# Counting edges with packed bank numbers and one-hots on ScalarE, and five steps of the graph part put in another order

## The chip, the cores and the metric

One core of one Trainium2 chip runs the whole program. The metric is the device time in microseconds, the median of the runs; lower is better. The engines of the core work on queues of their own and meet at semaphores: TensorE (PE, its weight loads PEld), VectorE (DVE), ScalarE (ACT), GpSimd (POOL), and SyncE (SP), which here only starts DMAs.

## The reference, cut to what matters

Four graph networks run one after the other on 512 nodes of width 768 and 8704 edges, each inside a residual sum and a layer norm:

```python
edge_index = jnp.stack([src, dst])
x = _layernorm(x + gat(x, 8 heads, then 1 head, edge_index))           # L0: attention on edges
x = _layernorm(x + rgat(x, edge_index, edge_type_3))                   # L1: 3 relations, 4 heads, then 1
x = _layernorm(x + rgcn(x, edge_index, edge_type_4))                   # L2: 3 layers, 4 relations
x = _layernorm(x + gcn(x, edge_index))                                 # L3: 2 layers
return x
```

In L0 a head computes `h = x @ W`, `e = leaky_relu(alpha_s[src] + alpha_d[dst])`, a softmax of e over the edges of each dst, and sums `h[src] * alpha` per dst. In L2 a relation's messages are divided by its in-degree: `norm = where(etype == r, 1 / max(deg[dst], 1), 0)`.

## The kernel before

The kernel never touches single edges after its first part. **Counting** (`count_and_weigh`, up to 106 us) turns the edge list into matrices that say how many edges of each kind go from source node to destination node. All later sums over edges are dense products with these 512 x 512 matrices.

Counting sorts the edges by source into 8 buckets of 64 sources and pads each bucket to chunks of 128 edges, 75 chunks in all (`CHUNKS`). For each chunk VectorE makes two one-hot matrices: `key_first` (128 edges x 128 keys, a piece of 15 chunks at a time, L382) and `dst_hot` (128 edges x 512 destinations, one chunk at a time, L433). TensorE multiplies them (L554) and adds the product to the PSUM bank of the chunk's bucket. Which bank that is depends on the data: VectorE counts it (L395 to L399) into `bank_i`, and TensorE's queue loads the numbers into registers, 8 at a time (`load_banks`, L535 to L540), each load four matmuls ahead of its use. There are three such rounds (`count_round`) over the same `dst_hot`, with other keys. Only the first waits for `dst_hot`, chunk by chunk. Between rounds ScalarE copies banks 0 to 4 and VectorE 5 to 7 out of PSUM (`tally`), and TensorE clears them with products of zeros (L543). During the rounds ScalarE does nothing else. A few late additions on VectorE (`total`, `most`) run beside round 3.

**The graph part** (`graph_layers`) begins with x transposed by TensorE (L1009). VectorE first copies six banks of the last round out (four named by `first_read`), then, in `turn`, subtracts ScalarE's rounded copy from each of six transposed pieces (`turn_hi`, `turn_lo`), so that a float32 product can be made of three products of rounded halves. The first product (L975, `product`) wants these. SyncE waits for all four `first_read` before it loads the second weight pass and stores `tally`.

Weights come in passes of three pieces. SyncE loads a piece into `w_raw` once POOL is done with the same piece of the pass before (`w_low`); ScalarE copies it rounded into `w_pair` (`split_high`), POOL subtracts (`weights_low`, L891). Each engine does its list in the written order, so a ScalarE copy of a tile waits behind a `split_high` whose load has not landed.

At the end of the first eight products TensorE transposes the largest count (`most`, L1192) into bank 7 for a flag that VectorE reads.

A **head** of L0 (`head`): TensorE makes the rows of the next head (8 products) and in between turns the source terms (`turn_source`, L989, bank 6), spreads them over partitions (`spread_source`, L993, bank 7), and, once VectorE has the maxima and the terms u and v (`uv_ready`), turns and spreads those (L984, L996, L997). Then it sums the probabilities (L1104) and makes six aggregations (L1114, 12 products of 512 columns each for the rounded and rest parts of rows and probabilities), each read by VectorE through a normalization and an elu. In the first head `late_weights` (L1027, L1038) stands in place of the output product, and `turn_late_weights` (L1061: 12 products of 8 columns) comes ahead of the aggregations. It waits for `wk_lo` of VectorE. ScalarE waits for its result before the elu copies. The eighth head has no next rows: its small steps stand between the chunks of the seventh head's output product (`eighth_head`, `out_by_chunk`, L1137), `source` after chunk 0 and `spread` after chunk 2 of 0 to 5, the turning of u and v after all.

In **L2** relation r's edge sums (L1535, L1543; `edge_sums`) are scaled by 1 over the in-degree. VectorE sums the rows of the count matrix (`count_sum`, three additions into `r_den`), TensorE sums over partitions (L1569, `degrees`), VectorE transposes and inverts it. For relation r + 1 the sum stands behind relation r's six tiles (`edge_tiles`, L2674) and behind the low part of the counts (`count_low`). ScalarE loads the next count matrix over the old one (`load_count`) once both are done, and splits the next two weight passes after that, before the copies of the next relation's tiles (`edge_high`). The edge sums use two PSUM banks and two `xt` buffers in turn.

## Time and profile before

| what | us |
|---|---|
| median of 3 runs (1712.0 to 1712.7) | 1712.49 |
| the profiled execution, its own time | 1713.1 |
| its span, first to last instruction | 1711.3 |
| TensorE busy | 1645.9 (96%) |
| VectorE busy | 1086.5 (63%) |
| ScalarE busy | 665.3 (39%) |
| GpSimd busy | 649.9 (38%) |
| mean granted clock of TensorE, as a share of full | 0.984 |

The profile is of one execution. Times in it count from the first instruction. A matmul's duration is longer than its pitch, since matmuls overlap; what one costs is the distance to the next start. Idle time is put down to the instruction that ended it.

### The profile page before, as it was taken

How to read it: one execution, taken by the hardware profiler on the slowest of the kernel's cores; microseconds unless marked ns; L12 is line 12 of the kernel's file. 1: busy time of each engine (PE TensorE's matmuls, PEld its weight loads, DVE VectorE, ACT ScalarE, POOL GpSimd, SP SyncE). 2: the span in 40 equal slices, each digit the busy share in tenths (PEclk: the TensorE clock that was granted, in tenths of full speed). 3: DMA queues.
4: the chain of work that ended last, by engine and by line, in shares of the span. 5: the costliest groups of instructions: out<-in, count | busy, mean ns of one | idle time of the engine just before them, and what ended most of it. 6: DMA issues, size and time to landing. Idle time of an engine off the chain costs nothing. (4 is left out here: it accounts for less than half of the span.)

```text
span 1711.3 us, 23130 instructions
## 1 busy us (share of the span) xinstructions
PE 1645.9 (96%) x8371; PEld 1416.7 (83%) x8371; DVE 1086.5 (63%) x2104; ACT 665.3 (39%) x1064; POOL 649.9 (38%) x606
## 2 busy tenths in 40 slices
PE   7899999999999999999998999899999999999998
PEld 4368699999999988789866998878888888999977
DVE  8746787787877877777699466844413331444646
ACT  1133544444344445434667443422233323332231
POOL 0033133423424233127677755323244324432421
PEclk9999999999999999999999999999999999999999
DMA  4155222422223232124100323112222222323231
GB/s 124 50 161 203 87 74 65 120 65 65 93 65 102 74 111 75 55 90 134 54 1 1 115 68 114 50 57 92 71 76 87 94 80 74 96 87 105 84 129 47
DMA packets 57178, 145.34 MB, mean 85 GB/s; under 512 B 13936, under 2 KB 17136, under 8 KB 56048
## 3 DMA queue, kind: packets, MB, share of 16 engines
q1 hardware_dynamic: 50448, 111.11, 21.2%
q10 hardware_dynamic: 6624, 32.77, 5.6%
q8 instruction: 73, 1.20, 0.3%
q14 instruction: 33, 0.27, 0.1%
HBM read 131.80 MB, written 12.06 MB: 84 GB/s over the span
## 5 line engine op out<-in xcount | busy, mean ns | idle before, releaser
L891 POOL TENSOR_TENSOR w_pair<-early,w_pair 128x384 fp32r<-128x384 f32 x468 | 490.7, 1087 | 900.4 <-ACT w_pair L1658 900.3
L975 PE MATMUL ps<-w_pair,cols_x 128*128 128x384 f32 x2088 | 376.8, 337 | 0.6 <-DVE al_part L2092 0.6
L975 PEld LDWEIGHTS ps<-w_pair,cols_x 128*128 128x128 f32 x2088 | 362.2, 188 | 6.3 <-issue 3.7
L975 PE MATMUL ps<-w_pair,wide 128*128 128x384 f32 x1728 | 303.0, 335 | 0.3 <-DVE early L2086 0.3
L975 PEld LDWEIGHTS ps<-w_pair,wide 128*128 128x128 f32 x1728 | 299.5, 188 | 3.5 <-issue 2.5
L1658 ACT ACTIVATE w_pair<-early 128x768 fp32r<-128x768 f32 x234 | 181.7, 838 | 306.8 <-PE ps L1595 140.3
L1595 PE MATMUL ps<-wide,w_pair 128*128 128x512 f32 x972 | 227.4, 392 | 3.0 <-DVE wide L2083 3.0
L1595 PEld LDWEIGHTS ps<-wide,w_pair 128*128 128x128 f32 x972 | 181.1, 188 | 43.2 <-DVE wide L2083 5.5
L1114 PE MATMUL ps<-prob,wide 128*128 128x512 f32 x576 | 138.2, 401 | 0.0
L1543 PE MATMUL ps<-prob,wide 128*128 128x512 f32 x546 | 137.1, 390 | 0.0
L1114 PEld LDWEIGHTS ps<-prob,wide 128*128 128x128 f32 x576 | 110.4, 192 | 26.3 <-issue 3.4
L2674 DVE TENSOR_TENSOR xt<-ps,multi 128x512 f32<-128x512 f32 x72 | 49.6, 691 | 112.2 <-PE ps L1543 110.8
L1543 PEld LDWEIGHTS ps<-prob,wide 128*128 128x128 f32 x546 | 102.1, 188 | 21.4 <-issue 0.2
L1658 ACT ACTIVATE wide<-ps 128x384 fp32r<-128x384 f32 (+1 forms) x131 | 66.1, 505 | 131.2 <-PE ps L975 127.7
L2086 DVE TENSOR_TENSOR early<-early,ps 128x384 f32<-128x384 f32 x104 | 56.5, 550 | 88.8 <-PE ps L975 76.7
L1698 ACT ACTIVATE xt<-xt,ks 128x512 f32<-128x512 f32 x96 | 69.0, 721 | 65.9 <-DVE xt L2170 65.1
L1658 ACT ACTIVATE wide<-xt 128x512 fp32r<-128x512 f32 x84 | 52.6, 631 | 97.5 <-DVE xt L2674 97.5
L2083 DVE TENSOR_TENSOR wide<-ps,wide 128x384 fp32r<-128x384 f32 (+2 forms) x83 | 48.9, 589 | 45.4 <-ACT wide L1658 39.1
L891 POOL TENSOR_TENSOR wide<-early,wide 128x384 fp32r<-128x384 f32 x48 | 49.7, 1047 | 70.7 <-ACT wide L1658 70.6
L2176 DVE SCALAR_TENSOR_TENSOR yt<-xt,multi 128x512 f32<-128x512 f32 x76 | 66.8, 880 | 14.2 <-ACT xt L1698 13.8
L1433 PE MATMUL ps<-prob,wide 128*128 128x512 f32 x288 | 75.2, 397 | 0.0
L2083 DVE TENSOR_TENSOR wide<-xt,wide 128x512 fp32r<-128x512 f32 x84 | 65.7, 782 | 4.1 <-ACT wide L1658 2.4
(327 smaller groups left out, 2163.4 us busy)
## 6 DMA issues: line engine op xcount, KB each, us to landing
early<-weights SPq DMA_DIRECT2D x246, 384.0 KB, 3.1
edge_mask<-counts ACTq DMA_DIRECT2D x13, 512.0 KB, 3.3
multi<-attn ACTq DMA_DIRECT2D x8, 768.0 KB, 4.5
kept<-early ACTq DMA_DIRECT2D x3, 1536.0 KB, 5.8
counts<-tally SPq DMA_DIRECT2D x12, 256.0 KB, 4.5
multi<-kept ACTq DMA_DIRECT2D x2, 1536.0 KB, 6.5
edge_mask<-masks ACTq DMA_DIRECT2D x5, 512.0 KB, 4.2
last_raw<-weights SPq DMA_DIRECT2D x6, 384.0 KB, 5.2
```

What stands on the lines that cost most here:

```text
L891: return nc.gpsimd.tensor_tensor(dst, whole, high.bitcast(F32), ALU.subtract)
L975: mm = nc.tensor.matmul(ps[:, m, 0:HW], left[:, a, k, m * P:(m + 1) * P], w_pair[:, slot_of[0], b, k, :], start=(k == 0 and a + b == 0), s ...
L1114: mm = nc.tensor.matmul(ps[:, 4 + f % 2, :], rows[parity][:, a, s, f * P:(f + 1) * P], prob[:, b, s, :], start=(s + a + b == 0), stop=(s = ...
L1433: mm = nc.tensor.matmul(ps[:, 2 * (h % 2) + c, :], rows[r][:, a, s, f * P:(f + 1) * P], prob[:, b, s, :], start=(begin and a + b == 0), st ...
L1543: mm = nc.tensor.matmul(bank, rows[0][:, a, s, f * P:(f + 1) * P], prob[:, 0, s, :], start=False, stop=(s + a == NB))
L1595: mm = nc.tensor.matmul(ps[:, SUM_BANK[f], :], w_pair[:, n, b, k, part], left[:, a, k, :], start=(begin and k + a + b == 0), stop=(end and ...
L1658: return nc.scalar.activation(dst, src, ACT.Copy)
L1698: nc.scalar.activation(xt[:, slot], xt[:, slot], ACT.Exp, bias=bias).then_inc(x_exp, 1)
L2083: return nc.vector.tensor_tensor(dst, a, b, ALU.subtract)
L2086: return nc.vector.tensor_tensor(dst, a, b, ALU.add)
L2176: nc.vector.scalar_tensor_tensor(y, xt[:, slot], 1.0, count, ALU.min, ALU.mult).then_inc(x_mid, 1)
L2674: nc.vector.tensor_tensor(xt[:, f % 2], ps[:, banks[f], :], scale, ALU.mult).then_inc(y_done, 1)
```

## The change

- Four bank numbers go into one value, base 8 (`PACKED`). TensorE's queue loads 19 such values once, ahead of the rounds, and takes a chunk's bank out of them with register arithmetic before its matmul (`bank_of`).
- ScalarE makes `dst_hot` of every fifth chunk in the first round: the square of (destination - node), then relu(1 - square). `neg_ready` tells that the destinations are there; TensorE waits for `fifth_ready` on these chunks and for a recounted `dst_ready` on the others.
- At the begin of the graph part VectorE's copies of banks 1 to 3 stand between pairs of `turn` subtractions.
- The transpose of `most` goes to bank 6 and waits for `mask_act` 2 in place of `mask_dve` 2; the waits of the first head's `turn_source` and `spread_source` are set to match.
- `turn_late_weights` follows the first aggregation.
- In the eighth head `spread` follows chunk 1 and the turning of u and v chunk 4.
- The row sum of relation 1's counts stands right behind the inverse in-degrees of relation 0, ahead of its tiles.

```diff
@@ -309,6 +317,16 @@
             copy(wkq[:, :, 0, 0:8], ps[:, 4, 0:8 * KB].rearrange("p (k v) -> p k v", k=KB)).then_inc(wkq_hi, 1)
+            act.wait_ge(neg_ready, 1)
+            for i in range(CHUNKS // 5 + 1):
+                if i < CHUNKS // 5:
+                    c = 5 * i + 4
+                    if i >= 2:
+                        act.wait_ge(fifth_ready, i - 1)
+                    nc.scalar.activation(square[:, i % 2], neg_node[:], ACT.Square, bias=neg_dst[:, c:c + 1], scale=-1.0).then_inc(squared, 1)
+                if i >= 1:
+                    act.wait_ge(squared, i)
+                    nc.scalar.activation(dst_hot[:, 5 * i - 1], square[:, (i - 1) % 2], ACT.Relu, bias=1.0, scale=-1.0).then_inc(fifth_ready, 1)
             for i in range(2):
@@ -393,10 +413,12 @@

-            step(nc.vector.tensor_tensor(past[:], chunk_f[:].unsqueeze(1).to_broadcast([1, BUCKETS - 1, CHUNKS]),
-                                         bases[0:1, 3, 4:3 + BUCKETS].unsqueeze(2).to_broadcast([1, BUCKETS - 1, CHUNKS]), ALU.is_ge))
+            step(nc.vector.tensor_tensor(past[:], chunk_f[:].unsqueeze(1).to_broadcast([1, BUCKETS - 1, CW]),
+                                         bases[0:1, 3, 4:3 + BUCKETS].unsqueeze(2).to_broadcast([1, BUCKETS - 1, CW]), ALU.is_ge))
             step(nc.vector.tensor_reduce(bank_f[:], past[:].rearrange("p k c -> p c k"), mybir.AxisListType.X, ALU.add))
-            nc.vector.tensor_copy(bank_i[:, 0:CHUNKS], bank_f[:]).then_inc(banks_ready, 1)
+            step(nc.vector.tensor_tensor(digits[:], digits[:], bank_f[:].rearrange("p (g j) -> p g j", j=PACKED), ALU.mult))
+            step(nc.vector.tensor_reduce(packed_f[:], digits[:], mybir.AxisListType.X, ALU.add))
+            nc.vector.tensor_copy(bank_i[:], packed_f[:]).then_inc(banks_ready, 1)
             dve.wait_ge(wkq_hi, 1)
@@ -405,7 +427,8 @@
             step(nc.vector.tensor_scalar(key3[:], sorted_fields[:, 1], -1.0, None, ALU.add))
-            later(nc.vector.scalar_tensor_tensor(neg_dst[:], dst_up[:], -grid(512.0), sorted_fields[:, 0], ALU.add, ALU.subtract))
+            nc.vector.scalar_tensor_tensor(neg_dst[:], dst_up[:], -grid(512.0), sorted_fields[:, 0], ALU.add, ALU.subtract).then_inc(neg_ready, 1)
+            dve.wait_ge(neg_ready, 1)
             nc.vector.tensor_scalar(kind3[:], key3[:], -31.5, grid(64.0), ALU.add, ALU.add).then_inc(decoded, 1)
@@ -430,7 +453,8 @@
                 for c in range(i * KEY_PIECE, (i + 1) * KEY_PIECE):
-                    nc.vector.tensor_scalar(dst_hot[:, c], neg_node[:], neg_dst[:, c:c + 1], None, ALU.is_equal).then_inc(dst_ready, 1)
+                    if c % 5 != 4:
+                        nc.vector.tensor_scalar(dst_hot[:, c], neg_node[:], neg_dst[:, c:c + 1], None, ALU.is_equal).then_inc(dst_ready, 1)
                 if i + 1 < KEY_PIECES:
@@ -532,29 +556,26 @@

-            def load_banks(first):
-                count = min(8, CHUNKS - first)
-                _, values = nc.values_load_multi_w_load_instructions(
-                    bank_i[0:1, first:first + count], engines=[mybir.EngineType.PE], min_val=0, max_val=BUCKETS - 1,
-                    skip_runtime_bounds_check_because="a count of seven comparisons")
-                return values
+            _, packed = nc.values_load_multi_w_load_instructions(
+                bank_i[0:1, :], engines=[mybir.EngineType.PE], min_val=0, max_val=BUCKETS ** PACKED - 1,
+                skip_runtime_bounds_check_because="four counts of seven comparisons each")
+
+            def bank_of(c, turn):
+                return ((packed[c // PACKED] + turn * BUCKETS ** PACKED) // BUCKETS ** (c % PACKED)) % BUCKETS

...

-            def count_round(keys, keys_ready, with_dst):
-                values, following = load_banks(0), None
+            def count_round(turn, keys, keys_ready, with_dst):
                 for c in range(CHUNKS):
-                    if c % 8 == 0 and c:
-                        values = following
                     if c % KEY_PIECE == 0:
                         pe.wait_ge(keys_ready, c // KEY_PIECE + 1)
-                    if with_dst:
-                        pe.wait_ge(dst_ready, c + 1)
-                    mm = nc.tensor.matmul(ps[:, bass.ds(values[c % 8], 1)], keys[:, c], dst_hot[:, c], start=False, stop=c == CHUNKS - 1,
+                    if with_dst and c % 5 == 4:
+                        pe.wait_ge(fifth_ready, c // 5 + 1)
+                    elif with_dst:
+                        pe.wait_ge(dst_ready, c - c // 5 + 1)
+                    mm = nc.tensor.matmul(ps[:, bass.ds(bank_of(c, turn), 1)], keys[:, c], dst_hot[:, c], start=False, stop=c == CHUNKS - 1,
                                           skip_group_check=True)
-                    if c % 8 == 3 and c - 3 + 8 < CHUNKS:
-                        following = load_banks(c - 3 + 8)
                 mm.then_inc(counted, 1)
@@ -573,9 +594,9 @@
                 if i == 0:
-                    count_round(key_second, second_keys, False)
+                    count_round(1, key_second, second_keys, False)
                 else:
-                    count_round(key_first, third_keys, False)
+                    count_round(2, key_first, third_keys, False)

@@ -1077,10 +1098,12 @@
                                 pe.wait_ge(rd_done, h)
+                            else:
+                                pe.wait_ge(flag_ready, 1)
                             turn_source()
...
                             if not with_last:
-                                pe.wait_ge(flag_ready, 1)
+                                pe.wait_ge(mask_dve, 2)
                             pe.wait_ge(q_ready, h * 2 + 1)
@@ -1102,9 +1125,6 @@
                 nc.tensor.matmul(ps[:, 6, :], ones[:].bitcast(F32), prob_sum, start=True, stop=True).then_inc(misc_done, 1)
-                if not with_last:
-                    turn_late_weights()
-
                 pe.wait_ge(rows_ready, h * 8 + 8)
@@ -1114,6 +1134,8 @@
                     mm.then_inc(agg_done, 1)
+                    if not with_last and f == 0:
+                        turn_late_weights()

@@ -1157,9 +1179,11 @@

-                out_by_chunk(h - 1, j, {0: source, 2: spread})
-                pe.wait_ge(uv_ready, h + 1)
-                turn_small(uvc_of[0], 4)
+                def turned():
+                    pe.wait_ge(uv_ready, h + 1)
+                    turn_small(uvc_of[0], 4)
+
+                out_by_chunk(h - 1, j, {0: source, 1: spread, 4: turned})
                 pe.wait_ge(q_ready, h * 2 + 2)
@@ -1188,8 +1212,8 @@
                 turn_last_masks(m)
-            pe.wait_ge(mask_dve, 2)
-            nc.tensor.transpose(ps[0:1, 7, 0:P], most[:], ident[:]).then_inc(most_turned, 1)
+            pe.wait_ge(mask_act, 2)
+            nc.tensor.transpose(ps[0:1, 6, 0:P], most[:], ident[:]).then_inc(most_turned, 1)
             pe.wait_ge(consts, 3)
@@ -2095,8 +2119,8 @@

-            def turn(count):
-                for f in range(KB):
+            def turn(count, begin=0, end=KB):
+                for f in range(begin, end):
                     dve.wait_ge(turn_hi, count + f + 1)
@@ -2210,9 +2234,10 @@
                 copy(tally[:, 4 + f], count_ps[:, 4 + f]).then_inc(middle_read, 1)
-            for m in range(NB):
+            copy(tally[:, 0], count_ps[:, 0]).then_inc(first_read, 1)
+            for m in range(1, NB):
+                turn(0, 2 * m - 2, 2 * m)
                 copy(tally[:, m], count_ps[:, m]).then_inc(first_read, 1)
-            turn(0)
             dve.wait_ge(consts, 1)
@@ -2332,7 +2357,7 @@
             dve.wait_ge(most_turned, 1)
-            mark(nc.vector.tensor_reduce(waited[0:1, :], ps[0:1, 7, 0:P], mybir.AxisListType.X, ALU.max))
+            mark(nc.vector.tensor_reduce(waited[0:1, :], ps[0:1, 6, 0:P], mybir.AxisListType.X, ALU.max))
             wait_steps()
@@ -2705,10 +2730,13 @@
                         dve.wait_ge(scale_ready, r + 1)
+                        if r == 0:
+                            dve.wait_ge(cnt_in, 16 * 6)
+                            count_sum(1)
                     edge_tiles(number, scale_bc[:, r], cols_y[r % 2])
...
                         count_low(number + 2)
-                        if number + 1 < REL4:
+                        if 1 <= number < REL4 - 1:
                             count_sum(number + 1)
```

## Rows read from the trace of the kernel before

**Rows 1.** Page, part 1, and TensorE's waits: who waited for whom, us, times, longest.
```profile
PE 1645.9 (96%) x8371; PEld 1416.7 (83%) x8371; DVE 1086.5 (63%) x2104; ACT 665.3 (39%) x1064; POOL 649.9 (38%) x606
...
PE ps L1104 <- DVE prob L2083: 4.5, 2, 3.0
PE ps L1569 <- DVE r_den L2086: 3.6, 1, 3.6
PE count_ps L554 <- issue: 1.6, 3, 0.8
PE ps L1192 <- DVE mask_rows L2325: 1.4, 1, 1.4
PE ps L996 <- ACT alpha L1658: 0.7, 1, 0.7
```

**Rows 2.** Windows: length, busy us and instructions by engine, PEclk, DMA share, GB/s.
```profile
62.60:69.10 6.50, 5.89 (x15) 2.00 (x15) 6.50 (x9) 0.00 (x0) 0.00 (x0) 0.50 0.67 161
69.10:82.60 13.50, 13.44 (x63) 5.88 (x60) 4.00 (x5) 0.03 (x1) 0.00 (x0) 1.00 0.20 79
188.50:195.40 6.90, 6.31 (x21) 5.54 (x22) 4.77 (x6) 0.31 (x2) 3.37 (x4) 0.51 0.58 171
659.57:663.00 3.43, 3.43 (x10) 2.66 (x9) 2.53 (x4) 0.85 (x1) 3.42 (x4) 0.50 0.60 213
1035.00:1038.40 3.40, 3.40 (x12) 3.40 (x11) 1.82 (x2) 1.73 (x4) 2.53 (x2) 0.51 0.00 0
1140.80:1147.70 6.90, 5.26 (x11) 3.49 (x12) 3.56 (x7) 2.31 (x3) 3.98 (x5) 0.51 0.32 100
```

**Rows 3.** VectorE's lines, 33 to 58 us: count, busy us, mean ns, idle before.
```profile
L433 DVE TENSOR_SCALAR dst_hot<-neg_node,neg_dst 128x512 f16<-128x512 f16 x75 | 20.1, 347 | 0.0
L382 DVE TENSOR_TENSOR key_first<-pos,key_pair 128x1920 f16<-128x1920 f16 x4 | 4.6, 1151 | 0.0
```

**Rows 4.** ScalarE's lines by shape, the whole span.
```profile
L1658 ACT ACTIVATE wide<-xt 128x512 fp32r<-128x512 f32 x84 | 52.6, 631 | 97.5 <-DVE xt L2674 97.5
L1704 ACT ACTIVATE yt<-yt,b_cols 128x512 f32<-128x512 f32 x35 | 24.8, 708 | 0.0
L295 ACT ACT_TABLE_LOAD x1 | 1.3, 1283 | 0.8 <-PEq L2797 0.8
```

**Rows 5.** Sources L537, L554, L1519, TensorE's sequencer: min/median/max ns, first and last.
```profile
L537 PEldq TENSOR_LOAD <-bank_i x30: 588/592/2307, 31.9 to 103.1; - x30
L554 PEldq FUSED_REGOPS  x225: 46/46/51, 33.4 to 104.7; - x113
L1519 PEldq FUSED_REGOPS  x1: 170/170/170, 1093.7 to 1093.7; - x1
```

**Rows 6.** Timeline of VectorE and ScalarE, 106 to 120 us: start, us, instructions.
```profile
106.67 3.68 DVE L2089 CAST tally<-count_ps 128x512 int16<-128x512 f32 x6 [7.95 <-PEq L111]
110.44 3.08 DVE L2083 TENSOR_TENSOR cols_x<-ps,cols_x 128x512 fp32r<-128x512 f32 x5
109.81 3.27 ACT L1658 ACTIVATE cols_x<-ps 128x512 fp32r<-128x512 f32 x6
119.05 0.85 ACT L1658 ACTIVATE w_pair<-early 128x768 fp32r<-128x768 f32 x1 [2.83 <-DMA early<-weights]
```

**Rows 7.** Timeline of TensorE around L1061 and at two lone waits.
```profile
189.09 2.69 PE L1061 MATMUL ps<-sel,wide 8*128 8x8 f32 x12 [1.69 <-DVE wide L2083]
903.41 0.49 PE L1367 MATMUL ps<-alpha,sel 48*128 48x512 f32 x1 [1.35 <-ACT early L1658]
1033.81 1.05 PE L1254 MATMUL ps<-ones,prob 128*128 128x2 f32 x8 [1.88 <-POOL prob L891]
```

**Rows 8.** Timeline of VectorE in the eighth head.
```profile
634.78 0.06 DVE L2138 MEMSET waited<- 128x1 f32 x1 [2.66 <-PE ps L993]
```

**Rows 9.** Timeline of ScalarE and TensorE in relation 1's edge sums.
```profile
1153.22 0.85 ACT L1658 ACTIVATE w_pair<-early 128x768 fp32r<-128x768 f32 x1 [1.00 <-DMA early<-weights]
1157.24 0.39 PE L1535 MATMUL ps<-prob,wide 128*128 128x512 f32 x1
```

More of the change, by code:

```diff
@@ L88 @@
 KEY_PIECES = 5
-SMALL_BYTES = 8672
+PACKED = 4
+SMALL_BYTES = 192 + 8672
 KEY_PIECE = CHUNKS // KEY_PIECES
@@ L129, in count_and_weigh @@
         edge_i = sb("edge_i", [P, 4, CH], I32)
+        digits = sb("digits", [1, CW // PACKED, PACKED], F32)
+        packed_f = sb("packed_f", [1, CW // PACKED], F32)
         edge_f = sb("edge_f", [P, 4, CH], F32)
@@ L146, in count_and_weigh @@
         warm = sb("warm", [P, 4], F32)
-        bank_i = sb("bank_i", [1, CW], I32)
+        bank_i = sb("bank_i", [1, CW // PACKED], I32)
         front = 2 * KB * N * 4 * 2
@@ L171, in count_and_weigh @@
         before_h = sb("before_h", [P, P], F16)
-        chunk_i = sb("chunk_i", [1, CHUNKS], I32)
-        chunk_f = sb("chunk_f", [1, CHUNKS], F32)
-        bank_f = sb("bank_f", [1, CHUNKS], F32)
-        past = sb("past", [1, BUCKETS - 1, CHUNKS], F32)
+        chunk_i = sb("chunk_i", [1, CW], I32)
+        chunk_f = sb("chunk_f", [1, CW], F32)
+        bank_f = sb("bank_f", [1, CW], F32)
+        with nc.sbuf_tensor("past", [1, BUCKETS - 1, CW], F32) as past:
+            pass
+        square = sb("square", [P, 2, N], BF16)
         key3 = sb("key3", [P, CW], F32)
@@ L209, in count_and_weigh @@
         dst_ready = sem("dst_ready")
+        neg_ready = sem("neg_ready")
+        squared = sem("squared")
+        fifth_ready = sem("fifth_ready")
         counted = shared["counted"]
@@ L289, in _ @@
             nc.gpsimd.iota(neg_i[:], pattern=[[-1, N]], base=0, channel_multiplier=0).then_inc(iota_done, 1)
-            nc.gpsimd.iota(chunk_i[:], pattern=[[P, CHUNKS]], base=0, channel_multiplier=0).then_inc(iota_done, 1)
+            nc.gpsimd.iota(chunk_i[:], pattern=[[P, CW]], base=0, channel_multiplier=0).then_inc(iota_done, 1)
         @block.scalar
@@ L332, in _ @@
             later(nc.vector.memset(column_sums[:], 63.5))
+            for j in range(PACKED):
+                later(nc.vector.memset(digits[:, :, j], float(BUCKETS ** j)))
             nc.vector.memset(bases[:], 0.0).then_inc(sums_ready, 1)
@@ L566, in _ @@
             clear(3)
-            count_round(key_first, first_keys, True)
+            count_round(0, key_first, first_keys, True)
             for i in range(2):
```

## The prediction, written before the changed kernel ran

> **What bounds the kernel now.** I read four views. The page's first part: TensorE is busy for 96% of the span, the next engine for 63%, so time is gained only where TensorE idles or runs at its lower clock. The waits of TensorE name the idle stretches, and six of them are what the diff touches: 3.0 us before the probability sum at L1104, 3.6 before the in-degrees at L1569, 1.7 before L1061, 1.6 of "issue" in the counting at L554, 1.4 before L1192, 0.7 before L996 [rows 1, 7]. The windows show the clock: after such a wait the granted clock is half, 1.2 of 2.4 GHz, for 3.4 to 6.8 us [rows 2]. A counting matmul then takes 0.43 us (15 in 6.5) and not 0.214 (63 in 13.5), so 6.8 us at half give away 3.4. The lines and the timeline give durations.
>
> **Counting, first round.** TensorE waits for `dst_hot`, which VectorE makes: 75 instructions in 20.1 us, 0.268 each, and one `key_first` per 15 of them (1.15 each, of which 0.15 overlaps) [rows 3]. The change leaves 60: 15 x 0.268 = 4.0 us off the path. ScalarE takes the 15 as Square and Relu. Neither is in the trace on this input; the nearest rows are 0.71 us for an activation with a column as bias and 0.63 for one without [rows 4]. A Square waits for the Relu issued just before it, so a pair costs about 1.35, at most 1.5; VectorE gives five chunks in 4 x 0.268 + 1.0/3 = 1.4. 15 pairs end near 31.9 + 0.6 + 20.3 = 52.8 us, VectorE near 53.9: hidden, with little to spare; at 1.5 it is 0.9 late. Were a table load needed, 1.28 us once [rows 4], it comes out of the 4.0 at worst. **-4.0** (-2.3 to -4.2). Two more small VectorE steps for packing and one wait lie in idle time before `routed`, or cost 0.05.
>
> Here the Trainium skill speaks against the change: ScalarE: Activation LUTs, "Rules for kernel authors", wants relu, max and multiply on VectorE and not on ScalarE. Instruction by instruction the trace agrees (0.27 against 0.71 + 0.63), and by the rule the 4.0 would be no gain; I don't follow it because ScalarE stands idle through the whole round.
>
> **Counting, bank numbers.** Before, one TENSOR_LOAD of 8 registers stands in TensorE's queue per 8 matmuls: 30 of them, median 0.59 us, up to 2.3 [rows 5]. Of these only two open a stall, 0.61 and 0.80 us at the start of rounds 2 and 3. With 19 packed numbers loaded once these go: **-1.4**. The one load of 19 costs 1 to 1.8 us ahead of the clears (0.59 for eight, so 1.8 as three loads, 1.0 if the fixed part is paid once; estimates from [rows 5]); clears then end up to 1.4 us later, and TensorE makes it up inside round 1, where it needs 0.216 per chunk and gets one per 0.28: 0.
>
> New is arithmetic per matmul: add, divide, remainder, address. Before there is one FUSED_REGOPS of 0.046 us per matmul [rows 5]. What it and the issue of the pair take is at most (8 x 0.214 - 0.59)/8 = 0.14 us, since TensorE ran without a gap beside the loads [rows 2, 5]. Lower bound 0: the same instruction holds the longer expression and stays under 0.216. Upper bound by the dearest such row, 0.170 at L1519 [rows 5]: 0.14 + 0.124 = 0.264, 0.048 too much on 150 matmuls, **+7.2** (round 1 hides it behind 0.28). I take 0, nearest to the 225 rows of the same line.
>
> **Clock in rounds 2 and 3.** Each starts with 6.8 us at half (from 62.2, and alike from 86.1, whose row is left out) [rows 2], and the load's stall falls in their first part. After the wait at 658.6, where no second wait followed, it was 3.4 us [rows 2]. So without the stall I expect one such stretch per round: 2 x 1.7 = **-3.4** (0 to -6.8).
>
> **Begin of the graph part.** VectorE now copies bank 0, then two subtractions, bank 1, two, bank 2, two, bank 3. Before: six copies from 106.67 (0.6 each), then the first subtraction at 110.44 [rows 6]. That one waits for ScalarE, which delivers `cols_x` at 110.4 [rows 6]; so it can't start earlier, and three copies are pushed in. The fifth subtraction ends at 114.75 instead of 113.5; the first product wants it at 114.4: +0.4. Also `first_read` reaches 4 at 115.9 and not 110.35, and SyncE waits for it ahead of load_pass(1), the stores of `tally` and pass 2: three weight loads start at 116.0 to 116.9 instead of 110.6 to 114.4. The last landed at 119.0 (ScalarE copy at 119.05, [rows 6]); with about 4.6 us it lands near 121.5, ScalarE's first tile copy goes from 119.8 to 122.4, VectorE's tile ends at 124.5, POOL's low part at 126.2, and the second pass wants them at 125.3 and 126.4. Just covered. **+0.4** (0 to +2).
>
> The transpose of `most` waits for `mask_act` 2, done at 137.1, and no longer for `mask_dve` 2: the 1.4 us before L1192 go [rows 1]. Next late is nothing: the flag (144.4) and `kc` are ready before TensorE wants them at 147. **-1.35** (-0.5 to -1.4).
>
> **First head.** The 12 small products now come behind the first of six aggregations. The 1.7 us wait goes, as `wk_lo` is long ready [rows 7]. The clock was at half from 188.5 to 195.4, so the 12 took 2.6 us for 1.3, and the aggregation from 191.7 gave away 1.85 more [rows 2, 7]. Before that stood two waits, 1.55 and 1.69 us; one stays. After a lone 1.35 (903.4) the clock stayed up, after a lone 1.88 (1033.8) it fell [rows 2, 7]. 1.55 is nearer to the first: -1.7 - 1.3 - 1.85 = **-4.8** (-1.7 if it falls anyway). ScalarE gets `wk_turned` at 193, before its first elu at 195.
>
> **Eighth head.** `spread` moves one chunk forward, so VectorE's maxima, which began 2.66 us late on L993 at 634.8 [rows 8], end 2.2 earlier; `turned` runs before the sixth chunk, which covers ScalarE's copy. The 0.7 us before L996 goes and the chain behind it moves with it; the 3.0 us before L1104 stay, as tiles and probabilities follow TensorE. **-0.7** (0 to -0.9).
>
> **In-degrees.** The sum for relation 1 (three adds, 2.1 us) moves to 1121.7, where VectorE idles 4 us. The 3.65 us before L1569 go, and the 2.6 that the half clock costs up to 1147.7 [rows 1, 2]. But ScalarE's queue holds: split of pass 46, then of pass 47, then the tile copies. Pass 46 began at 1142.8 after the sums; now it follows the low part of the counts, done at 1140.2: 2.1 us earlier. POOL, SyncE's loads and their landing hang on it; the third piece of pass 47, waited for until 1153.2, comes at 1151.1, and the first tile copy behind its 0.85 at 1151.9, not 1154.0 [rows 9]. The fifth edge sum wants the buffer which that frees, near 1153.9; it ran at 1157.24 [rows 9], and TensorE now gets there at 1150.4. So 6.3 us shrink to 3.3, and a new idle of 3.5 us stands there, long enough to lower the clock for 3.4 to 5.2 us, as at 658.6 and 1142.4: +1.9. **-1.4** (-0.7 to -6.3).
>
> **Sum.** -4.0 - 1.4 + 0 - 3.4 + 0.4 - 1.35 - 4.8 - 0.7 - 1.4 = -16.7 on the profiled execution's 1713.1 us (span 1711.3 and 1.8 around it): 1696.4. The median of the three runs is 0.6 lower: 1695.8, rounded to 1696.
>
> **The rivals.**
> 1. The clock doesn't follow my reading: the half stretches of rounds 2, 3 and of the first head stay as long. For it: their causes (clears after the read-out, 1.55 us) remain. Against: 3.4 us at 659.6. Costs 3.4 + 3.1: 1702.5. The Trainium skill, TensorE: Matmul & The Clock Gate, "Part 1", says that "the default state is throttled, and activity releases the throttle"; by it the new idle in the in-degrees brings the clock down again, and the trace agrees at 1140.8.
> 2. The register arithmetic costs 0.17 a matmul: TensorE's queue sets rounds 2 and 3, +7.2: 1703. It would show as even gaps and a half-idle load row.
> 3. More comes back: the clock stays up in rounds 2 and 3 (3.4 more) and behind the new idle in the in-degrees (1.9): 1690.5. For it: the stretches end as soon as TensorE runs without a wait.
> 4. Slower: the expression takes several instructions of 0.17. Two give 0.14 - 0.046 + 0.34 = 0.43 per matmul: 150 x 0.22 = 33 in rounds 2 and 3 and 75 x 0.15 = 11 in round 1, +44: 1740. It decides above 0.33 us a matmul, where 150 x 0.11 eats the 16.7. Against: 225 rows at 0.046.
> 5. The begin's late loads stall the second pass by 2 us and more; alone it only takes 1698.
>
> **Chances.** Forecast 0.50; rival 1 0.18; rival 2 0.14; rival 3 0.10; rival 4 0.04; rival 5 0.04. Range 1690 to 1705: it holds rivals 1, 2, 3 and 5 and leaves out rival 4 and combinations of 1 and 2. A measurement of this kernel tells 0.2%, 3.4 us, from no change. Faster 0.95, within it 0.01, slower 0.04.
>
> **What would show it.** `counted` 1 at 54.6 instead of 58.8; no TENSOR_LOAD inside the rounds and a 0.216 us pitch there; half clock of 3.4 us in each; no idle before L1192's successor, L1061's and L996's; `cols_x` subtractions with casts between; agg rows at full clock from 178 on; an idle of about 3.5 us at the fifth edge sum of relation 1. The prediction is wrong if matmuls in rounds 2 and 3 stand over 0.22 us apart at full clock, or if round 1 ends with TensorE waiting for ScalarE.

## The result, and the profile after

Twelve executions of the changed kernel have a median of 1702.65 us (1699.04 to 1712.22), twelve of the kernel before 1713.43 (1711.48 to 1718.25): ratio 0.9942, 95% interval 0.993 to 0.9955, faster by 0.58%. The forecast was 1696.0, within 1690 to 1705. The profiled execution took 1700.6 us (span 1698.6), 12.5 less than the one of before; the forecast for it was 16.7 less. The executions spread twice as far as those of before (13.2 us for 6.8), and the longest has the lowest mean granted clock, the shortest the highest: 0.978 at 1712.2, 0.989 at 1699.0.

The page's first part, and TensorE's waits (who waited for whom, us in total, times, longest), of the kernel after:
```profile
PE 1639.7 (97%) x8371; PEld 1416.4 (83%) x8371; DVE 1076.3 (63%) x2095; ACT 683.6 (40%) x1094; POOL 649.3 (38%) x606
```
```profile
PE ps L1127 <- DVE prob L2107: 4.5, 2, 3.0
...
PE count_ps L577 <- DVE dst_hot L457: 4.1, 4, 1.7
...
PE ps L1559 <- DVE xt L2699: 3.6, 4, 3.1
...
PE count_ps L567 <- issue: 0.8, 1, 0.8
```
Against [rows 1]: the waits at before's L1569, L1192 and L996, and the issue waits inside the counting (L554), are gone. L1127 is the old L1104, unchanged. New are 3.1 us at L1559 (the fifth edge sum of relation 1) and 0.8 of issue before the first clear (the load of 19 registers).

VectorE's and ScalarE's lines in round 1, then TensorE's sequencer (min/median/max ns), after:
```profile
L457 DVE TENSOR_SCALAR dst_hot<-neg_node,neg_dst 128x512 f16<-128x512 f16 x60 | 16.2, 347 | 0.0
...
L326 ACT ACTIVATE square<-neg_node,neg_dst 128x512 bf16<-128x512 f16 x15 | 10.7, 721 | 2.3 <-DVE neg_dst L430 1.9
L329 ACT ACTIVATE dst_hot<-square 128x512 f16<-128x512 bf16 x15 | 9.1, 613 | 0.0
```
```profile
L559 PEldq TENSOR_LOAD <-bank_i x1: 2037/2037/2037, 30.2 to 30.2; - x1
...
L577 PEldq FUSED_REGOPS  x225: 89/124/141, 34.1 to 94.9; - x113
```
VectorE makes 60 in 16.2 us where [rows 3] have 75 in 20.1. ScalarE needs no table load here and finishes a pair every 1.27 us. One FUSED_REGOPS per matmul still does the arithmetic; it takes 124 ns, not the 46 of [rows 5], and the load of all numbers 2.04 us, not 1 to 1.8.

Windows of after (length, busy us and instructions of PE, PEld, DVE, ACT, POOL, then the granted clock, DMA share, GB/s):
```profile
59.20:63.40 4.20, 4.20 (x13) 1.60 (x13) 4.20 (x8) 0.00 (x0) 0.00 (x0) 0.59 0.82 198
63.40:76.90 13.50, 13.50 (x64) 6.08 (x62) 6.50 (x6) 0.00 (x0) 0.00 (x0) 1.00 0.28 95
80.40:83.80 3.40, 3.40 (x10) 0.98 (x9) 0.67 (x1) 0.00 (x0) 0.00 (x0) 0.51 0.70 151
104.33:107.74 3.41, 3.41 (x13) 3.41 (x13) 3.41 (x7) 1.23 (x3) 3.12 (x7) 0.50 0.00 0
178.50:198.50 20.00, 19.81 (x89) 15.77 (x90) 15.69 (x24) 10.21 (x19) 5.63 (x6) 1.00 0.20 60
1141.98:1145.39 3.41, 3.41 (x10) 2.64 (x9) 1.74 (x4) 0.80 (x2) 0.00 (x0) 0.50 0.38 115
1626.68:1633.50 6.82, 6.15 (x15) 4.08 (x14) 4.25 (x7) 1.92 (x4) 0.00 (x0) 0.50 0.42 144
```
Against [rows 2]: 64 counting matmuls fill 13.5 us at full clock, 0.21 each, so the 124 ns of arithmetic hide behind them. Rounds 2 and 3 start with 3.4 us at half and not 6.8. The first head runs at full clock. But the clock is at half in two places where it was not before, at 104.3 and at 1626.7, and the diff touches nothing near the second.

**Segments.** To see which of this is the change, I cut each trace at the starts of named matmuls: the first `dst_hot` (VectorE), the 75th and 225th counting matmul, the transpose of `most`, the probability sums of heads 1, 2, 7 and 8, the first in-degree sum, that of relation 2, the last matmul. "Others" are the profiles of the section below whose kernels hold that part as the changed kernel does.

| segment (us) | before, two profiles | after | others with that part | forecast | measured |
|---|---|---|---|---|---|
| start to first `dst_hot` | 32.87, 32.80 | 33.63 | 32.3 to 34.4 | 0 | chance |
| round 1 | 25.59, 25.62 | 21.56 | 21.55 to 21.57 (22.18 with single bank numbers) | -4.0 | -4.05 |
| rounds 2, 3 with read-outs | 47.51, 47.11 | 43.27 | 44.8 to 45.0 in eight, 43.3 in one | -4.8 | -2.1 to -4.2 |
| to `most` | 36.12, 36.10 | 36.06 | 35.1 to 35.3, or 36.0 | -0.95 | -0.9 or -0.1 |
| to head 1's probability sum | 44.19, 44.19 | 43.97 | 43.97 to 44.01 | 0 | -0.2 |
| first head | 75.95, 75.90 | 71.87 | 71.88, 71.89 | -4.8 | -4.05 |
| heads 2 to 6 | 347.90, 347.90 | 347.90 | 347.90 | 0 | 0 |
| eighth head | 48.45, 48.46 | 47.75 | 47.74 to 47.76 | -0.7 | -0.70 |
| to the first in-degrees | 460.5, 463.7 | 460.6 | 459.1 to 469.7 | 0 | chance |
| in-degrees | 62.15, 62.22 | 60.76 | 60.56 to 60.84 | -1.4 | -1.5 |
| the rest | 524.2, 524.0 | 525.4 | 523.7 to 525.6 | 0 | see below |

Most segments repeat to some hundredths; heads 2 to 6, where TensorE never idles, to the last digit shown. What varies stands where TensorE idles, above all the stretch of 460 us that the change doesn't touch: 10.6 us between profiles.

The gaps between the starts of counting matmuls split what rounds 2 and 3 gained. At half clock they are 0.43 us; in the kernel before one gap of each round, the fourth, was 1.24 and 1.43, in its second profile 0.72 and 1.21. So the loads' stalls cost 1.8 and 1.1 us in the two profiles. The idle that the profile names is a little less than the growth of the gap (TensorE's timeline of before, rounds 2 and 3):
```profile
65.10 10.10 PE L554 MATMUL count_ps<-dst_hot,key_second 128*128 128x512 f16 x37 [0.61 <-issue]
...
88.83 17.52 PE L554 MATMUL count_ps<-dst_hot,key_first 128*128 128x512 f16 x71 [0.80 <-issue]
```
After the change no gap in these rounds is over 0.43.

### The profile page after: what moved, and what is told of

Its sections match the earlier page's. It is cut to its first block and busy times, and to the rows that moved or that the text cites. A ratio compares the mean times of both kernels' runs of the same rounds, so it can differ in the third digit from the quotient of the medians.

```text
span 1698.6 us, 23123 instructions
## 1 busy us (share of the span) xinstructions
PE 1639.7 (97%) x8371; PEld 1416.4 (83%) x8371; DVE 1076.3 (63%) x2095; ACT 683.6 (40%) x1094; POOL 649.3 (38%) x606
## 5 line engine op out<-in xcount | busy, mean ns | idle before, releaser
L996 PE MATMUL ps<-w_pair,cols_x 128*128 128x384 f32 x2088 | 377.9, 338 | 0.6 <-DVE al_part L2116 0.6
L996 PEld LDWEIGHTS ps<-w_pair,cols_x 128*128 128x128 f32 x2088 | 363.6, 189 | 5.9 <-issue 3.4
L996 PE MATMUL ps<-w_pair,wide 128*128 128x384 f32 x1728 | 303.0, 335 | 0.3 <-DVE early L2110 0.3
L996 PEld LDWEIGHTS ps<-w_pair,wide 128*128 128x128 f32 x1728 | 299.5, 188 | 3.4 <-issue 2.5
```

The source lines that it names most:

```text
L996: mm = nc.tensor.matmul(ps[:, m, 0:HW], left[:, a, k, m * P:(m + 1) * P], w_pair[:, slot_of[0], b, k, :], start=(k == 0 and a + b == 0), s ...
```

## The experiments

Times are compared by their ratios to the kernel before on the same chip. The segments say more than the times, which scatter by more than most parts are worth: the intervals of most kernels with one part undone overlap with those of the changed kernel, and there the segments alone decide.

**The changed kernel, unedited, and the kernel before, unedited** (a second profile of each)

> The changed kernel, nothing edited: a second profiled execution of it. In the first one the clock fell to half at 104.3 us and at 1626.7 us, behind idles of TensorE that the kernel before has too (1.0 and 1.9 us, 1.3 to 0.4 us), where it did not fall; together 3.0 us. Theory (chance of the execution): the half-clock stretches lie elsewhere in this second profile, at least one of those two is gone, and waits of the same length are followed by half clock in one execution and not in the other; the executions spread over 10 us or more, as 1699 to 1712 did, with a lower mean clock in the longer ones. Rival (the change moves the idles so that these two stretches are its price): both stand again at the same places with the same lengths, and 3.0 of the 4.2 us that the forecast of 1696 missed belong to the change.

> The kernel before, nothing edited: a second profiled execution of it. Theory: its half-clock stretches also move; the long ones behind the clears (6.8 us from 62.2 and 86.1) may be 3.4, and the start (weights of the first head's queries, first transpose at 9.8 us) differs by some tenths. Rival: the same stretches to a few tenths of a microsecond in place and length.

The changed kernel: 1701.91 us (1699.05 to 1705.1), ratio 0.9934 (0.992 to 0.9947). The kernel before: one execution, 1715.62 us. The stretches at half clock, by the traces' clock record (start:length, us):
```
before    34.9:3.4 62.2:6.8 86.1:6.8 188.5:6.8 659.6:3.4 744.9:6.8 936.0:3.4 1035.0:3.4 1099.9:6.8 1140.8:6.8 1710.9:2.5   = 57.2
before 2  34.4:3.4 61.7:6.8 85.6:6.8 188.0:6.8 659.0:3.4 744.3:6.8 904.8:3.4 935.5:3.4 1034.5:10.2 1102.7:6.8 1143.7:6.8 1710.3:5.6   = 70.5
after     60.0:3.4 80.4:3.4 104.3:3.4 647.0:3.4 732.4:6.8 923.5:3.4 1022.5:3.4 1087.4:6.8 1142.0:3.4 1626.7:6.8 1698.4:2.6   = 46.9
after 2   35.4:3.4 59.3:3.4 79.7:6.8 646.4:3.4 711.2:10.2 738.5:3.4 926.2:3.4 1090.1:6.8 1144.7:3.4 1629.4:3.4 1697.7:5.1   = 52.9
```
The same code in the two profiles of the changed kernel, behind the same wait (1.3 us before the block sums, L1313): first the second profile, then the first.
```profile
711.20:721.40 10.20, 10.20 (x38) 9.80 (x37) 5.27 (x7) 0.63 (x1) 0.00 (x0) 0.50 0.00 0
```
```profile
710.45:720.65 10.20, 10.20 (x71) 9.93 (x70) 8.47 (x14) 4.33 (x6) 2.94 (x4) 1.00 0.00 1
```
38 matmuls at half clock or 71 at full, with no idle in either: one kernel, two executions. The stretch at 104.3 is absent here, too. The one near 1627 came back, and there the theory of chance does not hold: behind the same waits (1.3 and some of 0.4 us) it stands in all six profiles, of these and the kernels below, that have the new idle in the in-degrees, and in none of the eight without that idle, both of before among them. Between the two places TensorE is at work for 480 us. So it goes with the change's in-degree part; how, no run shows. The last segment has a mean of 524.6 with it and 524.2 without.

The Trainium skill, TensorE: Matmul & The Clock Gate, "Part 1", says that how many matmuls run at the lower clock at a kernel's start varies from run to run. Further in, these two profiles show the same: 46.9 and 52.9 us at half.

**All one-hots on VectorE**
```
-    if c % 5 != 4:
-        nc.vector.tensor_scalar(dst_hot[:, c], ...)
+    nc.vector.tensor_scalar(dst_hot[:, c], ...)          # ScalarE's Square and Relu removed
```


> The changed kernel with all 75 one-hots of dst back on VectorE and none on ScalarE. Theory: 15 x 0.262 to 0.268 us return on the path of round 1: from the first key_first to the last dst_hot 26.0 us and not 22.1, and the time rises by 4 us against the changed kernel (ratio 1.0023). Rival (round 1 is set by something else, as TensorE's arithmetic of 0.124 us a matmul or the later clears): below 2 us. Rounds 2 and 3 keep pitch 0.216.

1708.12 us (1702.09 to 1712.35), ratio 0.9965 (0.9953 to 0.9977). VectorE's line in round 1 there:
```profile
L446 DVE TENSOR_SCALAR dst_hot<-neg_node,neg_dst 128x512 f16<-128x512 f16 x75 | 20.1, 352 | 0.0
```
Round 1 takes 25.25 and not 21.55: 3.7 us on the path. VectorE's stretch from the first `dst_hot` to the last takes 24.66 and not 20.73, 3.93 or 15 x 0.262. That is still 0.35 below the 25.6 of the kernel before: this rest of the gain in round 1 comes from something else in the change, and the next experiment points at the packing. The median rose by 6, 2 more than round 1 explains; in the profile the untouched middle is long, too (466.3 for 460.6 and 463.2).

**One bank number per chunk, loaded by eights**
```
-    _, packed = nc.values_load_multi_w_load_instructions(bank_i[0:1, :], ...)
+    values = load_banks(0)      # then load_banks(c + 5) at every c % 8 == 3
```


> The changed kernel with one bank number per chunk, loaded eight at a time, as before. Theory: the stalls in the first matmuls of rounds 2 and 3 (0.8 and 1.0 us over the pitch) return and with them some half clock, 1.8 to 5 us in the two rounds together, forecast 4.8; the stall of 0.8 us ahead of the clears of round 1 goes, and gives back nothing, as VectorE sets that round. The packing on VectorE costs 0. Rival: the register arithmetic of the packed numbers costs what the loads cost, and the time stays within 1 us.

1707.6 us (1704.95 to 1714.33), ratio 0.9959 (0.9946 to 0.9972). Rounds 2 and 3 with read-outs take 47.7 us, with packed numbers 44.9 as a rule: 2.8. The fourth gaps are back (1.46 and 1.47 us), 2.1 of the 2.8. Round 1 takes 22.18 for 21.56, which I had not expected: a load of 0.78 us at 53.6 holds the 69th of its 75 matmuls back by 0.67, too near the end to be made up. The kernel before has the same gap at the same matmul (0.96 us where its neighbours have 0.26). So the packing pays in round 1 as well.

**The late weights' products back in front of the aggregations**
```
+    if not with_last:
+        turn_late_weights()
     pe.wait_ge(rows_ready, h * 8 + 8)
```


> The changed kernel with the 12 small products of the late weights in front of the six aggregations of the first head again. Theory: their wait of 1.7 us returns behind the 1.55 us of the probability sum, and after the two the clock may fall, as before: +1.7 to +4.8 us against the changed kernel, where 4.2 to 4.5 were gained in the profiles. If the clock stays up behind the two waits in this execution, +1.7 to +2.2. Rival (the products behind the first aggregation only move the wait elsewhere): within 1 us.

1705.35 us (1702.89 to 1708.14), ratio 0.9949 (0.9935 to 0.9962). The first head takes 76.25 us and not 71.88, 4.4 more, and the clock falls behind the two waits as in both profiles of before:
```profile
182.30:189.10 6.80, 6.80 (x22) 5.73 (x22) 4.33 (x5) 0.31 (x2) 2.41 (x3) 0.50 0.52 169
```
It fell 3 times of 3 with two waits, and in none of the 11 profiles with one.

**The in-degree sum of relation 1 behind the tiles again**
```
-    if r == 0:
-        dve.wait_ge(cnt_in, 16 * 6)
-        count_sum(1)
```


> The changed kernel with the in-degree sum of relation 1 behind the tiles of relation 0 again. Theory: the idle of 3.65 us before the in-degrees returns, the one of 3.07 before the fifth edge sum of relation 1 goes: net +1.4 us against the changed kernel (0.7 to 3). Rival (the new idle has another cause): it stays, and the time rises by 5 us or more.

1705.0 us (1702.38 to 1710.48), ratio 0.9937 (0.9923 to 0.9952). The wait for the in-degrees is back, that at the fifth edge sum gone:
```profile
PE ps L1593 <- DVE r_den L2110: 3.6, 1, 3.6
```
The segment takes 62.18 and not 60.6 to 60.8: the move is worth 1.5. The rival, another cause for the new idle, is out.

**Order of copies, wait before `most` and eighth head as before**
```
+    for m in range(NB): copy(tally[:, m], ...)
+    turn(0)
...
+    pe.wait_ge(mask_dve, 2)                # for mask_act, 2; bank 7 for 6
...
+    out_by_chunk(h - 1, j, {0: source, 2: spread})
```


> The changed kernel with three small parts undone, far apart in the trace: VectorE's copies and subtractions at the begin of the graph part in the old order, the wait and bank of the transpose of most as before, and the eighth head's steps as before. Theory, read part by part: the order of the copies 0 (0 to -0.4 us), the wait ahead of most back with 1.35, the wait of 0.7 in the eighth head back; +1.6 to +2.1 us in all, which the time alone hardly shows, and the waits do. Rival: the late start of the weight loads behind the new order of copies had a cost, and undoing it gives 1 us or more.

1705.05 us (1700.18 to 1708.67), ratio 0.9939 (0.9922 to 0.9956). The waits returned as expected: to `most` 36.11, to the first probability sum 44.18, eighth head 48.46. The order of copies is not free, though: the last product before `most` starts 32.9 us after the counting with the old order (four profiles without a fall of the clock) and 33.3 to 33.5 with the new (five), about +0.5. In the changed kernel VectorE pushes three copies between the subtractions:
```profile
104.14 0.68 DVE L2113 CAST tally<-count_ps 128x512 int16<-128x512 f32 x1
104.74 1.28 DVE L2107 TENSOR_TENSOR cols_x<-ps,cols_x 128x512 fp32r<-128x512 f32 x2
105.94 0.68 DVE L2113 CAST tally<-count_ps 128x512 int16<-128x512 f32 x1
```

**ScalarE's splits of pass 47 between the tile copies** (run twice)
```
 copy(dst[:, 0, f, :], xt[:, f % 2]).then_inc(y_hi, 1)
+if f < 3: split_piece(47, 1, f)            # relation 1, first layer
```


> The changed kernel, but ScalarE's three splits of weight pass 47 stand between the tile copies of relation 1 (one behind each of the first three) and no longer ahead of all. Theory (the new idle of 3.07 us before the fifth edge sum comes from ScalarE, which waits for the third piece of pass 47, landed at 1138.2, before it copies the first tile): the first tile copy comes near 1133.9, right behind VectorE's tile, the idle goes, and with it the half clock that follows: -3.1 to -4.8 us against the changed kernel. Rival 1: the load of pass 47 itself is then waited for by the second half of the column product: 1 us or less gained. Rival 2: the tiles or counts of VectorE are late in their own right: the idle shrinks to 1 to 2 us and the clock falls all the same.

> The changed kernel with the moved splits of pass 47 alone, again, on the same chip as the one with added work: for comparison with it. Theory: 1697 to 1701 us, in-degree segment 55.8 us as before (60.6 to 60.8 without the moved splits), executions spread over 6 us and more. Rival (the 1698.9 measured first was a lucky set): 1701 or more, as the changed kernel.

1698.92 us (1695.33 to 1701.06), ratio 0.9904 (0.9888 to 0.992); again 1698.95 (1698.73 to 1699.92), ratio 0.9912 (0.9896 to 0.9929). Timeline of ScalarE (start, us, instructions, what ended its idle), changed kernel, then with the moved splits:
```profile
1134.18 0.85 ACT L1682 ACTIVATE w_pair<-early 128x768 fp32r<-128x768 f32 x1 [3.71 <-DMA early<-weights]
1136.27 0.85 ACT L1682 ACTIVATE w_pair<-early 128x768 fp32r<-128x768 f32 x1 [1.24 <-DMA early<-weights]
1138.22 0.84 ACT L1682 ACTIVATE w_pair<-early 128x768 fp32r<-128x768 f32 x1 [1.10 <-DMA early<-weights]
1138.97 1.13 ACT L1682 ACTIVATE wide<-xt 128x512 fp32r<-128x512 f32 x2
```
```profile
1138.25 0.63 ACT L1682 ACTIVATE wide<-xt 128x512 fp32r<-128x512 f32 x1 [3.39 <-DVE xt L2708]
1138.79 0.83 ACT L1682 ACTIVATE w_pair<-early 128x768 fp32r<-128x768 f32 x1
1140.01 0.63 ACT L1682 ACTIVATE wide<-xt 128x512 fp32r<-128x512 f32 x1 [0.39 <-DVE xt L2708]
```
And TensorE at the fifth edge sum, the same two kernels:
```profile
1136.72 1.75 PE L1567 MATMUL ps<-prob,wide 128*128 128x512 f32 x7
1141.54 0.50 PE L1559 MATMUL ps<-prob,wide 128*128 128x512 f32 x1 [3.06 <-DVE xt L2699]
```
```profile
1140.89 0.39 PE L1559 MATMUL ps<-prob,wide 128*128 128x512 f32 x1
1141.12 1.75 PE L1567 MATMUL ps<-prob,wide 128*128 128x512 f32 x7
1142.71 0.39 PE L1559 MATMUL ps<-prob,wide 128*128 128x512 f32 x1
```
The profile names VectorE as the one TensorE waited for. But VectorE itself waited for ScalarE, whose queue held three splits, each waiting for its weight load, ahead of the copy of a tile. With the splits between the copies the idle goes, and the half clock behind it: the segment takes 55.77, 4.9 less. That is shown, by an edit that moves nothing else.

The second profile of this kernel shows the other cost of the new begin of the graph part: the second weight pass comes 0.64 us late, and `most` at 36.0:
```profile
115.81 4.67 PE L996 MATMUL ps<-w_pair,cols_x 128*128 128x384 f32 x26
121.12 1.15 PE L996 MATMUL ps<-w_pair,cols_x 128*128 128x384 f32 x5 [0.64 <-DVE al_part L2125]
```

**The old order of copies besides**

> The kernel with the moved splits of pass 47, and besides VectorE's copies and subtractions at the begin of the graph part in the old order. Between the last counting matmul and the transpose of most the profiles show 36.1 us with the old order and the old wait, 35.2 with both new (36.05 where the clock fell in between), and the move of the wait alone should give 1.35 to 1.6. Theory (the new order costs 0.4 to 0.5 us in the first product): 34.6 to 34.8 there, without a fall of the clock, and 0.5 us off the time, under what the times can tell. Rival (the order costs nothing, the wait gave only 0.9): 35.2 again.

1700.95 us (1696.76 to 1706.09), ratio 0.9929 (0.9908 to 0.995). Not decided here: the clock fell at 104.9 and `most` comes after 36.05, as with the new order where it falls. The next kernel has the old order too, without a fall, and 34.71: 0.4 to 0.5 less than 35.1 to 35.3. The time, 2 us above that with the new order, tells nothing at this scatter.

**Work in TensorE's idles** (edits to that kernel)
```
 clear(b)
+if b < ACT_BANKS: clear(b)
...
+for _ in range(keep_busy.get(m, 0)):       # {2: 6, 3: 16} and {3: 12}
+    nc.tensor.transpose(ps[:, 4, m * P:(m + 1) * P], ident[:], ident[:])
 pe.wait_ge(acc_ready, ready + m + 1)
...
 pe.wait_ge(vb_ready, h + 1)
+for _ in range(10): nc.tensor.transpose(ps[:, 6, 0:P], ident[:], ident[:])
 pe.wait_ge(den_sum, 3 * h + 3)
```


> The same kernel, with transposes and clears on TensorE whose results are overwritten, put into idles that end at other engines: five banks are cleared twice between the counting rounds, 6 and 16 transposes of the identity stand before the third and fourth wait of the turn after the eighth head, 12 before the fourth in the one after the relational part, 10 before the last probability sum. Theory (idle of TensorE is what lowers its clock, and the clock is what the executions differ in): the idle at these places shrinks by 1 to 2 us each, the half-clock stretches behind them (3.4 to 6.8 us behind each in all profiles so far) get shorter or go: rounds 2 and 3 together 33 to 34 us where they took 35.0 to 36.4, the stretches at 647 and 733 gone; -3 to -7 us against the kernel without them. Rival 1 (the clock falls for another reason, as the data or the moment): the same stretches, 0 us. Rival 2: the added work delays what it stands ahead of: slower by up to 2 us.

1697.82 us (1696.43 to 1698.48), ratio 0.9905 (0.989 to 0.9919). Two places did nothing or harm. The doubled clears left rounds 2 and 3 at 45.4. Before the probability sum the added ten stood behind the wait that ends last, so they came on top (1.7 us; the eighth head took 49.47):
```profile
647.22 1.92 PE L1132 MATMUL ps<-ident 128*128 128x128 f32 x10 [2.97 <-DVE prob L2123]
648.94 1.91 PE L1134 MATMUL ps<-early,ones 128*128 128x512 f32 x2
```
The two turns did what was expected; the next kernel repeats them.

**The same without those two, and with work before the block sums and the row sums**
```
+if x_base == 80 and s == 0: 10 transposes into ps[:, 5, 384:512]     # block_sums
+if late is not None and s == 1: 7 products there, start=False        # row_sums
```


> The kernel with the moved splits and the old order of copies, with added work on TensorE only where its wait stands last: 6 and 16 transposes before the third and fourth wait of the turn after the eighth head, 12 before the fourth of the turn after the relational part, 10 before the first wait of the block sums after the last weights (idle of 1.3 us, behind which the clock falls in 5 of the 12 profiles so far for 10.2 or 6.8 us), 7 products before the second wait of the relational row sums (idle of 1.9 us). The two places where the added work gave nothing, the clears and the last probability sum, are without it. Theory (idle lowers the clock, where and how often is chance): the turn after the eighth head takes 20.6 us and not 22.15, the one after the relational part 9.0 and not 9.2 to 9.6, no fall at 711 us, and the last probability sum no longer comes 1.7 late: 1693 to 1697 us, and executions that lie closer together than the 9 us of the kernel without the added work. Rival (other idles take over the falls, as one at 712 did): no gain over it, 1698 to 1701.

1694.83 us (1693.85 to 1697.16), ratio 0.989 (0.9872 to 0.9907), the fastest here: 4.1 below the moved splits alone on the same chip, no execution of the one reaching the other's, though the intervals of the ratios overlap a little (0.9896 to 0.9907); the old order of copies is a second difference between the two. Windows around the turn after the eighth head, in the kernel with the old order of copies and no added work, then with the 22 transposes:
```profile
729.69:733.00 3.31, 0.89 (x5) 0.42 (x4) 2.91 (x8) 0.20 (x1) 0.00 (x0) 1.00 0.00 0
733.00:739.80 6.80, 5.83 (x26) 5.83 (x27) 4.72 (x8) 3.60 (x7) 0.00 (x0) 0.50 0.76 308
```
```profile
729.90:733.20 3.30, 2.92 (x26) 2.65 (x25) 2.85 (x9) 0.20 (x1) 0.00 (x0) 1.00 0.00 0
733.20:740.00 6.80, 6.00 (x42) 5.35 (x41) 4.50 (x8) 3.26 (x6) 0.00 (x0) 1.00 0.79 308
```
TensorE does 2.92 us of work where it did 0.89, the wait ends at nearly the same moment, and the clock stays up: from the first to the last of the turn's 24 transposes it takes 6.9 us in both kernels with added work. Without added work the clock fell there in 11 of 12 profiles, and the same took 7.75 to 8.43; in the twelfth, where it stayed up, 6.9. So the clock is all that the added work gave at this place. The 24 transposes after the relational part take 5.8 to 5.9 and not 6.1 to 6.5, with 3.4 us at half behind them where 9 of 12 have 6.8. (The expectation's figures for both turns are of longer segments.) Behind the two newly filled waits the clock didn't fall; of the 13 profiles without that work it fell in 5 behind the first (1.3 us, before the block sums) and in 9 right behind the second (1.9 us, before the row sums). In all TensorE spent 29.8 us at half clock; the others have 43 to 74. Not all is gain: the clock fell for 6.8 us at 890, and the segment to the first in-degrees, which holds all four places, took 460.6 where the changed kernel's first profile has the same without any added work, and the ten profiles of changed kernels without it have 459.1 to 469.7. That work in an idle keeps the clock up is borne out at the first turn; how much of the 4.1 us it made is open. The Trainium skill, TensorE: Matmul & The Clock Gate, "Part 1", says that "activity releases the throttle"; the two windows at 733 agree.

## Why the prediction was right, and by how much each step missed

The direction was right and the time within 0.4%. Read in segments, as most profiles show them, the terms sum to -13.8 (-4.05 - 2.4 - 0.9 - 0.2 - 4.05 - 0.7 - 1.5), forecast -16.7; the times give -10.8. So two thirds of the forecast gain came, and every part of it is there, most of them near their forecast size; rounds 2 and 3 are the exception.

- **Round 1**, -4.0: -4.05. ScalarE's pairs took 1.27 for the 1.35 estimated. With all on VectorE again round 1 grew by 3.7; the other 0.35 the forecast gave to the one-hots, and it is not theirs. That the sum fits to 0.05 is luck.
- **Load stalls and register arithmetic**, -1.4 and 0: the loads were worth 1.8 and 1.1 us in the two profiles of before, so -1.4 is their mean, though it was read from one profile's idle times (0.61 and 0.80) where the gaps had grown by 0.81 and 1.00. The arithmetic hides. It was nearer to rival 2 than the choice of "nearest to the 225 rows of the same line" told: 0.124, not 0.046, and 0.14 + (0.124 - 0.046) = 0.218 against 0.216. The bound of 0.170 was the better row.
- **Clock in rounds 2 and 3**, -3.4: the term that was mis-sized. "One such stretch per round" held in 2 of 11 profiles with packed numbers, the profiled one among them; the other nine have 3.4 us in one round and 6.8 in the other. So of the three stretches that rival 1 wanted to stay, one stayed, 1.7 of its 6.5 us. With the stalls the rounds gave -2.4 as a rule and -4.2 in the profiled run, for -4.8.
- **Begin**, +0.4, and **`most`**, -1.35: -0.9 for the two, forecast -0.95. "Just covered" was right for the loads, and just: in one profile they came 0.64 late.
- **First head**, -4.8: -4.05. Wait and clock went as forecast. By the starts, the wait and the probability sum ahead of it gave 2.3 us, the 12 products 1.1 and the aggregations 0.7, where the forecast has 1.7, 1.3 and 1.85: the aggregations are the part that was mis-sized. Their seven gaps of 0.43 are gone, but a few others are longer than the usual 0.23: one of 0.63 behind the first aggregation product, and 0.57 and 0.34 at 186.97 us, where TensorE now arrives earlier and waits 0.19 for VectorE's `yt`. The forecast asked what is late next only for the wait it removed. Its rule that a lone wait as long as 1.88 us brings the clock down was one execution's: of the 13 profiles with that same wait the clock fell right behind it in 9. That it stayed up behind the 1.55 held in 11 of 11.
- **Eighth head**, -0.7: -0.70.
- **In-degrees**, -1.4: -1.5, with 3.07 us of new idle forecast as 3.5 and 3.4 us at half behind it. Its cause, ScalarE's queue, is shown by the edit that removes it.
- **Not foreseen**: the 3 us between -13.8 and -10.8. Ten profiles of kernels with the change or most of it, and no work added in these stretches, against two of before put 3.1 there: the start 33.3 for 32.8, the untouched middle 464.5 for 462.1, the end 524.4 for 524.1. With two profiles of before and a middle that varies by 10.6 this is a sum and no proof; the cause of the 3 us stays open. The forecast took every stretch at half clock outside the diff as fixed; they are not, from one execution to the next, and one (1627) went with an edit 480 us ahead of it.

## What to carry to other kernels

Cut the traces at named instructions and compare segments before the times: parts worth 0.5 us show there, where medians scatter by 3. Ask of a wait not only who released it, but what that engine waited for, and what stood in the queue of the next: here a split that waited for a load held back a tile that was ready. On TensorE an idle cost its length and, in some executions and not in others, up to half of 3.4 to 10.2 us more; work whose result is overwritten can fill it, if it stands ahead of the wait that ends last.

## What the runs showed of the hardware that was not expected

- The same instructions behind the same wait ran at half clock for 10.2 us in one execution and at full in another; in 14 profiles the time at half was 29.8 to 74.4 us, of which up to half is lost. Where TensorE never idled (heads 2 to 6, 347.90 us) all 14 agree.
- One register load of 19 numbers took 2.04 us, more than three loads of eight at their median together (3 x 0.59).
- Add, divide and remainder by powers of eight stayed one instruction per matmul, 0.124 us (median; 0.089 to 0.141) for 0.046.
- A stretch at half clock near 1627 us came in 6 of 6 profiles with an idle at 1141 and in 0 of 8 without it.
